# Thirteen products of constants on TensorE around the change from the gated cell to the shared experts

## The reference, cut to what matters

```
x = x + tanh(g_xattn[0]) * cell(layernorm(x), ctx, ctx, ...)     # ends with a norm over each token
x = x + tanh(g_ffn[0]) * moe(layernorm(x), ...)
...
# in moe, for each of two shared experts, over all tokens:
shared = shared + (silu(x @ w1.T) * (x @ w3.T)) @ w2.T
```

## Time and profile before

| what | value |
|---|---|
| median of the runs | 854.54 us |
| the profiled execution's own time | 852.18 us |
| its span, first to last instruction | 850.4 us |
| mean granted TensorE clock | 0.969 |
| TensorE matmul busy | 772.2 us, 91% |
| VectorE, ScalarE, GpSimd busy | 505.8, 399.9, 227.1 us |

### The profile page before, as it was taken

One profiled execution on the slowest core, in us unless ns is written; L12 is line 12 of the kernel. 1 busy time (PEld: TensorE's weight loads), 2 busy tenths in 40 slices (PEclk: granted clock), 3 DMA queues, 4 the chain that ended last, 5 costly groups with the idle time before them and its releaser, 6 DMA issues.

```text
span 850.4 us, 15258 instructions
## 1 busy us (share of the span) xinstructions
PE 772.2 (91%) x5380; PEld 627.3 (74%) x5380; DVE 505.8 (59%) x1159; ACT 399.9 (47%) x817; POOL 227.1 (27%) x208
## 2 busy tenths in 40 slices
PE   8587399999999999999999789997779999999997
PEld 7466287788887888888887455655558888888886
DVE  5588865465584333343343687978766665756644
ACT  5597545144462222322223598778645344243232
POOL 0079110037601232332234157664310000000000
PEclk9979699999999999999999999999999999999999
DMA  8478740033243334433332600202004023050140
GB/s 310 142 261 293 287 160 1 1 101 143 82 181 74 63 63 68 76 76 65 66 51 26 224 2 14 87 2 75 1 2 101 0 47 80 0 126 1 29 98 25
DMA packets 37513, 74.47 MB, mean 88 GB/s; under 512 B 4449, under 2 KB 25569, under 8 KB 35681
## 3 DMA queue, kind: packets, MB, share of 16 engines
q1 hardware_dynamic: 30288, 64.16, 24.4%
q0 software_dynamic: 7152, 9.34, 6.0%
HBM read 59.76 MB, written 19.01 MB: 93 GB/s over the span
## 4 chain that ended last, share of the span: by engine, by line
PE 54%; DVE 16%; ACT 8%; issue 4%; DVEq 4%; DMA 2%; ACTq 0%; POOLq 0%; SPq 0%
PE t_y_ps L2273 8%; PE f_y L1773 4%; PE a_turned L997 3%; ACT a_hhi L1163 2%; PE a_score L975 2%; PE a_score L977 2%; PE a_score L976 2%; PE t_up L2253 2%; PE t_up L2255 2%; PE t_up L2254 2%; PE t_gate L2243 2%; PE t_gate L2244 2%; PE a_proj L874 2%; PE t_gate L2245 2%; PE t_h_turned L2262 2%
## 5 line engine op out<-in xcount | busy, mean ns | idle before, releaser
L2213 POOL DMA_INDIRECT sums<-t_y,t_dest x39 | 60.9, 1560 | 169.2 <-DMA sums<-t_y,t_dest 121.0
L2308 ACT CAST t_xT_hi<-t_x_turned 128x256 fp32r<-128x256 f32 x39 | 14.5, 372 | 138.9 <-PE t_x_turned L2234 138.9
L2273 PE MATMUL t_y_ps<-W,t_hidT 128*128 x312 | 73.8, 379 | 0.8 <-ACT t_hidT L2318 0.8
L1163 ACT CAST a_hhi<-a_hid 128x512 fp32r<-128x512 f32 x48 | 29.8, 620 | 85.4 <-DVEq L1448 83.8
L2273 PEld LDWEIGHTS t_y_ps<-W,t_hidT 128*128 128x128 f32 x312 | 59.1, 190 | 10.5 <-issue 1.0
L1450 DVE TENSOR_TENSOR a_hlo<-a_hid,a_hhi 128x512 fp32r<-128x512 f32 x48 | 33.2, 692 | 35.2 <-ACT a_hhi L1163 35.2
L1152 ACT ACTIVATE a_act_g<-a_score 128x512 f32<-128x512 f32 x48 | 28.6, 596 | 47.7 <-PE a_score L977 47.3
L830 POOL TENSOR_TENSOR a_sc<-a_sc,a_nmx 128x512 f32<-128x512 f32 x32 | 33.3, 1042 | 56.6 <-DVE a_nmx L1296 56.6
L2337 DVE TENSOR_TENSOR t_hid<-t_act_g,t_up 128x512 f32<-128x512 f32 x39 | 28.1, 720 | 34.1 <-ACT t_act_g L2313 30.3
L1112 ACT ACTIVATE a_pr<-a_sc,a_nmx 128x128 f32<-128x128 f32 x128 | 40.8, 391 | 14.2 <-DVE a_nmx L1296 13.4
L1293 DVE TENSOR_TENSOR a_sc<-a_score,a_pen 128x1024 f32<-128x1024 f32 x32 | 38.9, 1217 | 4.3 <-PE a_score L889 3.2
(11 more groups left out here) (422 smaller groups left out, 2286.9 us busy)
## 6 DMA issues: line engine op xcount, KB each, us to landing
W<-in_w_dram SPq DMA_DIRECT2D x9, 1536.0 KB, 8.2
a_cb<-comb_rows SPq DMA_DIRECT2D x16, 512.0 KB, 7.6
W<-m_rows SPq DMA_DIRECT2D x14, 512.0 KB, 4.9
slot_tokens<-in_blank_rows_dram SPq DMA_DIRECT2D x1, 5031.0 KB, 20.1
t_x<-slot_tokens SPq DMA_DIRECT2D x39, 129.0 KB, 2.4
a_raw<-in_w_dram SPq DMA_DIRECT2D x3, 1536.0 KB, 6.3
X<-in_x_dram SPq DMA_DIRECT2D x4, 512.0 KB, 5.9
ctxT_all<-in_ctxT_dram SPq DMA_DIRECT2D x4, 512.0 KB, 8.6
```

The lines of the kernel that those rows point to most:

```text
L1163: act.copy(hhi[u % 2][:], hid[u % 2]).then_inc(hhi_ready, 1)
L2213: pool.indirect_dma_start(sum_dram, bass.IndirectOffsetOnAxis(ap=dest[p][:, 0:1].bitcast(U32), axis=0), y[p][:], None, compute_op=ALU.add) ...
L2273: last = pe.matmul(y_ps[p][:, 0:D], hidT[p][:, h], W[:, ds(e, 1), at:at + D], start=(h == 0), stop=(h == HT - 1))
```

## The change

Six products of the identity with 512 columns of constants are put at the end of TensorE's list in `cell`, five at the head of its list in the next block, ahead of the first turning, and two between that turning and `gate_up(0)`. Nobody reads what they write, and they wait for no semaphore and set none.

```diff
--- before.py
+++ after.py
@@ -447,6 +447,8 @@
                     turn_back(i - 1)
                 values(i)
             turn_back(PAIRS - 1)
+            for _ in range(6):
+                pe.matmul(pvT[0][:], cst[:, C_ID:C_ID + 128], cst[:, 0:512], start=True, stop=True)
 
         @block.scalar
         def _(act):
@@ -1775,8 +1777,14 @@
                                              start=first, stop=(n == U - 1 and part == 1), skip_group_check=True)
                 last.then_inc(h_used, 1)
 
+            def busy(n):
+                for _ in range(n):
+                    pe.matmul(y_bank[0][:], cst[:, C_ID:C_ID + 128], cst[:, 0:512], start=True, stop=True)
+
+            busy(5)
             turn(0, 0)
             turn(0, 1)
+            busy(2)
             gate_up(0)
             for u in range(NU - 1):
                 gate_up(u + 1)
```

## The result

22 runs of each kernel: before 853.83 us (849.55 to 857.34), after **850.59 us** (848.22 to 858.67). The ratio is 0.9968, with a 95% interval from 0.9953 to 0.9983: faster by 0.3%, or 2.7 us. A second comparison of the two gave 0.9959 [0.9940, 0.9978]. The profiled execution took 849.40 us with a span of 847.6, against 852.18 and 850.4.

A forecast was written before the change was run, and what follows sets the result against it. Nearly all of the stretch was taken to hang on VectorE and ScalarE, with TensorE at 1.2 GHz in the turning and most of gate_up(0). Sum: -2.12 at silu(0) + 0.33 at the barrier = -1.8 us; 854.54 to 852.7, range 848.8 to 856.0.

The forecast's parts named there:

- Cost of one product: Each added float32 product on TensorE takes 0.86 us at full clock and 1.72 at the low one.
- The six cost 0.33 us at the barrier: At the cell's end the six products end at 94.26, 0.33 us after VectorE's 93.93, delaying everything behind the barrier by 0.33.
- The five are hidden: Ahead of the turning the five products run from 94.6 to 98.9, with 1.8 us to spare before 100.74.
- The turning: At full clock ScalarE's first copy begins 0.49 us sooner, its second ends at 102.22 not 102.96; gate_up(0) is due 0.64 sooner.
- The two have 0.05 us of room: Between turning and gate_up(0) the two products run from 101.33 to 103.05; a miss costs its own length, 0.1 or so.
- The table load is late next: At silu(0), ScalarE's table load ends last, at 106.48 instead of 107.12, while TensorE would be ready at 106.02.
- 2.12 us at silu(0): silu(0), behind gate_up(0), starts at 106.50 instead of 108.62, 2.12 us won.
- Does the clock hold over the idle stretch?: Whether full clock survives TensorE's 1.8 us of idling before the turning; forecast about one half, a fall there 0.17.
- Rows 8: Profile rows where the clock fell near 80.4 although the idle stretches ahead were 1.34 us and, still running, 0.72 us.
- What is won at silu(0) is kept: Behind silu(0) each piece releases the next, up to one 3.10 us load at 257.77, so the gain should be kept.
- More is won than counted: Rival, chance 0.18: typical runs before lose more at low clock than the profiled one; 849 to 850 us against 854.54.

The follow-up runs named there:

- three: The changed kernel with three instead of five products ahead of the turning: 853.53 us, ratio to before 0.9985 [0.9956, 1.0013].
- ten_end: The changed kernel with ten instead of six products at the cell's end: 855.03 us, ratio to before 1.0015 [0.9993, 1.0038].
- six_five: The changed kernel without the two products between turning and gate_up(0), six and five kept: 852.71 us, ratio to before 0.9992 [0.9966, 1.0018].
- six_only: The changed kernel with only the six products at the cell's end, without the five and the two: 852.71 us, ratio to before 1.0002 [0.9973, 1.0031].
- five_two: The changed kernel without the six products at the cell's end, five and two kept: 851.15 us, ratio to before 0.9985 [0.9959, 1.0010].

## Why the prediction was right

The direction, the mechanism and the size of the main term held; the measured 850.59 us lies within the range, 2.1 us below the predicted 852.7. Of these, 0.7 is the kernel before, whose 22 runs have a median of 853.83 and not 854.54, 1.4 the change: a gain of 2.7 to 3.2 us by the timed runs where I forecast 1.8. By its steps:

- **Cost of one product.** 0.86 us predicted; the six span 5.32 us with the last one's tail, 5.15 + 0.17. Right, at both clocks: the two took 3.62 at the low one where the clock had fallen (the kernel three).
- **The six cost 0.33 us at the barrier.** The mechanism is right (ten_end), the term was mis-sized: it measured 0, not in the profiled execution alone, where they began 1.37 us sooner than assumed, but in all ten profiles with the six (or their time in transposes), where TensorE ended 0.35 to 1.47 us ahead of VectorE.
- **The five are hidden.** Right: 98.86 predicted 98.9.
- **The turning.** 0.49 and 0.74 us sooner for ScalarE's copies. From the barrier: the second copy began 8.14 us behind it before and 7.32 after, 0.82 sooner. Right within 0.1.
- **The two have 0.05 us of room.** They cost nothing, as six_five shows; they ran until gate_up(0)'s start, which came 8.81 us behind the barrier instead of 9.50, 0.69 sooner where 0.64 was predicted.
- **The table load is late next.** Right, and shown twice: silu(0) 0.01 us behind the load's end, and silu(0) at TensorE's end once the load was moved.
- **2.12 us at silu(0).** 2.19 from the barrier.
- **Does the clock hold over the idle stretch?** I gave it one half. It held over that stretch in all seven profiles with five products (or their time in transposes) there. I took the one stretch ahead of the turning for the place of danger. Rows 8 themselves had two stretches close together, and in six_five, where a second stretch lies close behind this one, the clock fell in the second. The rule of the Trainium skill that stands beside it in the prediction (TensorE: Matmul & The Clock Gate, "Why this matters for your kernels"), that only a gap well longer sends the clock down, does not hold in six_five either, where it fell in a stretch of 1.56 us behind one of 1.64.
- **What is won at silu(0) is kept.** In the pair of traces, 2.19 from the barrier is 2.1 at 255 us and 1.8 at 450. The prediction's words that the chain has one transfer are wrong: behind the one at 257.77 it has four more between 453 and 471 us in the trace before, and with them the distance of the two executions moved by 1.1 us.

That the gain came out at 2.7 to 3.2 us and not at 1.8 is explained by these steps only up to 2.2; what the timed runs show beyond it stays open. "More is won than counted" said that runs before the change may lose more at the low clock than the profiled one. The profile of six_only is one such case: its clock was still at 0.50 between 107 and 108, where the trace before had 0.66, and silu(0) came 0.37 us later behind the barrier. A few tenths can come from there; that it does in a typical run isn't shown. The interval, 0.17 to 0.47%, or 1.5 to 4.0 us, holds 2.2 without it.

## What to carry to other kernels

Filling TensorE's idle time with products of constants pays only up to the first work whose end the chain waits for. Fill it without leaving a second gap close behind a first: in the one execution that was profiled without the cheap two products beside the real work, 2.1 of the 2.2 us were lost, and the two cost nothing. Put the filler where another engine ends last, and count its length against that engine's end, since the barrier waited for the filler too. Once the clock is lost, the same filler costs twice its time and can make the work later than with none.

## What the runs showed of the hardware

- The barrier between the two blocks opened 0.30 to 0.32 us behind whichever engine ended last: VectorE in twelve profiles, TensorE with its last product done in one (ten_end).
- 104 float32 transposes held the granted clock, full when they began, at 1.00 from 88 to 104 us, with idle stretches of 1.3 and 1.6 us among them (one profile). The Trainium skill (TensorE: Matmul & The Clock Gate, "Part 4: PE-mode transpose") says that the full clock doesn't engage for them; this trace does not agree.
- The same idle length, 1.6 us, had no fall in it ahead of the turning in seven profiles and had one ahead of gate_up(0), directly behind the turning, in one (six_five).
- From the end of TensorE's last work to the fall of the clock it was 0.5 us in six_five, 1.5 in the kernel before, 2.2 in six_only, 2.3 in three and 3.8 in five_two.
- Two products cost 3.62 us at the low clock against 1.88 at full clock, tail included.
